# Second feed-forward: where ScalarE normalises the group three ahead

## The reference

```
x = x + 0.5 * ffn(layernorm(x))              # ffn: x @ w + bias, w = quantised kernel + a @ b
# and then, for the router of the experts, on layernorm(x):
ri = concat(xf, mean, std, min, max, l2, share of |x| < 1e-6)
h = gelu(ri @ r1_w.T + r1_b);  probs = softmax(h @ r2_w.T)
```

## Time and profile before

| | us |
|---|---|
| median of 3 runs | 1660.39 |
| lowest and highest | 1659.22, 1662.93 |
| the profiled execution | 1666.03 |
| its span, first to last instruction | 1664.2 |
| the stage of the change, in the span | about 570 to 683 |
| mean granted clock of TensorE | 0.906 |

### The profile page before, as it was taken

One profiled execution on the slowest core, in us unless ns is written; L12 is line 12 of the kernel. 1 busy time (PEld: TensorE's weight loads), 2 busy tenths in 40 slices (PEclk: granted clock), 3 DMA queues, 4 the chain that ended last, 5 costly groups with the idle time before them and its releaser, 6 DMA issues. The chain is left out here.

```text
span 1664.2 us, 26073 instructions
## 1 busy us (share of the span) xinstructions
PE 1402.3 (84%) x9264; PEld 1053.8 (63%) x9264; DVE 960.6 (58%) x2915; ACT 684.0 (41%) x1640; POOL 627.1 (38%) x573
## 2 busy tenths in 40 slices
PE   6889979999999778447999999499995459999995
PEld 5667544555554455226988899366663349888895
DVE  8987756777775488784542112266676855521120
ACT  4222147666666377434522232114333525322221
POOL 6652112221213243304435755422211232636655
PEclk9989879999999899658999999799996569999998
DMA  3034493333210023314777997611113326969985
GB/s 112 20 138 147 130 171 62 86 61 86 57 32 2 1 89 114 155 22 136 232 220 241 235 309 178 142 36 51 51 48 115 103 66 197 266 200 270 264 232 91
DMA packets 115534, 215.10 MB, mean 129 GB/s; under 512 B 20455, under 2 KB 80524, under 8 KB 106509
## 3 DMA queue, kind: packets, MB, share of 16 engines
q1 hardware_dynamic: 88526, 181.30, 34.5%
q0 software_dynamic: 26880, 32.13, 12.4%
HBM read 160.69 MB, written 52.30 MB: 128 GB/s over the span
## 5 line engine op out<-in xcount | busy, mean ns | idle before, releaser
L1072 DVE TENSOR_REDUCE attnm_top<-psum 128x1 f32<-128x63 f32 (+7 forms) x512 | 200.2, 449 | 65.4 <-PE psum L1153 62.8
L1295 ACT ACTIVATE attnm_prob<-psum 128x512 f32<-128x512 f32 (+1 forms) x384 | 189.7, 529 | 69.4 <-PE psum L1164 62.7
L2472 POOL DMA_INDIRECT out<-moe2e_y,moe_scatter_i x80 | 125.0, 1563 | 106.9 <-DMA out<-moe2e_y,moe_scatter_i 51.7
L2472 POOL DMA_INDIRECT x_sum<-moe1e_y,moe_scatter_i x80 | 125.3, 1566 | 106.0 <-DMA x_sum<-moe1e_y,moe_scatter_i 60.7
L2671 DVE SCALAR_TENSOR_TENSOR moe1e_h<-moe1e_gate,psum 128x160 f32<-128x160 f32 x160 | 50.5, 321 | 186.1 <-ACT moe1e_gate L2609 186.0
L2671 DVE SCALAR_TENSOR_TENSOR moe2e_h<-moe2e_gate,psum 128x160 f32<-128x160 f32 x160 | 50.5, 321 | 185.7 <-ACT moe2e_gate L2609 185.6
L2541 PE MATMUL psum<-moe2e_xgT,moe_w_up 128*128 128x160 f32 x1024 | 148.9, 303 | 0.8 <-ACT moe2e_xgT L2618 0.8
L2541 PE MATMUL psum<-moe1e_xgT,moe_w_up 128*128 128x160 f32 x1024 | 148.7, 302 | 0.8 <-ACT moe1e_xgT L2618 0.8
L2541 PEld LDWEIGHTS psum<-moe2e_xgT,moe_w_up 128*128 128x128 f32 x1024 | 143.9, 192 | 3.5 <-issue 2.5
L2541 PEld LDWEIGHTS psum<-moe1e_xgT,moe_w_up 128*128 128x128 f32 x1024 | 143.7, 192 | 3.5 <-issue 2.5
L1473 POOL DMA_INDIRECT moe_xg<-xn_rows,moe_gather_i x80 | 84.6, 1058 | 160.7 <-DVE moe_gather_i L1661 93.4
(11 more groups left out here) (435 smaller groups left out, 3134.7 us busy)
## 6 DMA issues: line engine op xcount, KB each, us to landing
moe_w_up<-in_expert_up SPq DMA_DIRECT2D x64, 1024.0 KB, 7.7
moe_w_down<-in_expert_down SPq DMA_DIRECT2D x64, 512.0 KB, 7.4
attnm_q_hat<-q_parts SPq DMA_DIRECT2D x72, 128.0 KB
moe_a_up<-in_adapter_up SPq DMA_DIRECT2D x32, 256.0 KB, 7.7
q_parts<-attnf_q_part SPq DMA_DIRECT2D x12, 512.0 KB, 2.8
attnm_k_hat<-k_parts SPq DMA_DIRECT2D x72, 64.0 KB
x_res<-in_x SPq DMA_DIRECT2D x8, 512.0 KB, 8.2
v_tails<-attnf_v_tail SPq DMA_DIRECT2D x8, 512.0 KB, 3.2
```

Source lines behind the costliest of these rows:

```text
L1072: ins = nc.vector.tensor_reduce(top[:, n // QUADS % 2, tile, hh:hh + 1], s.ps[:, u.bank, first:end], AX_X, ALU.max)
L1295: nc.scalar.activation(prob[:, i % NPROB, at:GROUP], s.ps[:, u.bank, at:GROUP], ACT.Exp).then_inc(taken[u.bank], 1)
L2472: nc.gpsimd.indirect_dma_start(total, bass.IndirectOffsetOnAxis(ap=scatter_i[:, at:at + 1], axis=0), y[:, q, k, :], None, bounds_check=TOK ...
```

## The change

In ScalarE's loop of `ffn_router`, `norm(i + 3)` stands directly behind `copy(i + 2)`, ahead of the router's work of the turn, instead of between `copy_x(i - 1)` and `gelu(i - 2)`. Nothing else is changed.

```diff
                 if 0 <= i + 2 < GROUPS:
                     copy(i + 2)
+                if 0 <= i + 3 < GROUPS:
+                    norm(i + 3)
                 if 0 <= i - 1 < GROUPS:
                     r.absolute(act, i - 1)
                     r.under(act, i - 1)
...
                     r.copy_s(act, i - 2)
                 if 0 <= i - 1 < GROUPS:
                     r.copy_x(act, i - 1)
-                if 0 <= i + 3 < GROUPS:
-                    norm(i + 3)
                 if 0 <= i - 2 < GROUPS:
                     r.gelu(act, i - 2)
```

## The result

| | median us | lowest, highest | runs |
|---|---|---|---|
| before | 1660.39 | 1656.73, 1662.93 | 9 |
| changed | 1665.27 | 1662.64, 1669.25 | 9 |

The ratio is 1.0041, with a 95% interval of 1.0028 to 1.0054: slower, by 4.6 to 9.0 us as the ratio has it and by 4.9 between the medians. The forecast was 1665.4. In a second job, with its own runs of the kernel before, the unedited changed kernel gave 1.0024 (1.0006 to 1.0042).

The account below looks back on a forecast made before the run. A closed ACT-PE round bounds the stage, no engine alone. C(5) at 612.0, then two turns of 12.64 + 1.54 us, put C(7) 5.0 us late: median 1660.39 becomes 1665.4, range 1660.0 to 1668.4.

Parts of the forecast that it names:

- The round: Second feed-forward with router: ACT to PE and back takes 10.57 us a turn, 12.64 with the normalisation ahead of copy_s.
- Turn 1: Group 4's normalisation fits in ACT's 3.80 us wait for DVE; C(4), its copy, comes 4.1 us earlier.
- Turn 2: Group 5's copy, C(5), at 612.0 against 613.49 before, with PE waiting 3.2 us for DVE's statistics.
- last two small operations: End of DVE's statistics of group 0: bias(5) may hold them; up to 1.2 us are covered before copy_s.
- two cases: C(5) at 610.9 with PE at full clock, or 613.1 with all behind PE's wait at half clock.
- Turns 3 and 4 and the clock: Each round lasts 12.64 us plus 1.54 for PE's fall to half clock after 2.95 us idle; C(7) 5.0 us late.
- the row with 2.94 us of waiting: PE's idle stretch before 656.86: clock fell from 2.4 to 1.2 GHz, L1938 took 3.50 us instead of 1.96.
- C: Rival: DVE paces the turns, so losing its clash with POOL gains up to 8.2 us, 1652.2; chance 0.06.
- D: Rival: the loss is taken up behind C(7), where ACT waits 2.35 us a turn; 1660.4 us, chance 0.08.
- B: Rival: PE's clock holds, C(7) is 0.8 us late, 1661.2 us, no difference that can be told; chance 0.28.

Follow-up runs that it names:

- Half the dose: The changed kernel with only tiles 0 and 1 of each group normalised ahead, 2 and 3 in the old place; turns 11.67 and 11.54 us, no ratio.
- a version with two other edits: Kernel before with groups 4, 5 normalised ahead, PE's row transposes first, POOL's powers before the bias add, router transposes repeated on PE; ratio 0.9974.

## Why the prediction was right, and where its terms were off

**The round.** Right. 0.91 + 3.89 + 0.81 + 4.96 closes without the normalisation, and with it ahead of copy_s the turn lasts 12.53 us; the sum said 12.64. Of the 0.11 us, 0.09 is that Abs starts 1.98 behind the start of L2144, not 2.07, when it need not wait (610.63 to 612.61): the term should have been the distance between the starts, not the duration. Half the dose gives half, a place behind copy_s gives nothing.

**Turn 1.** Right. C(4) is 9.64 us behind C(3) where it was 13.78, a lead of 4.1.

**Turn 2.** The total agrees, 612.0 against 609.72 + 2.50 = 612.22 on the clock of before, but in part by luck. PE's wait was put at 3.2 us and was 3.93. The "last two small operations" of the statistics were held by bias(5), L1857 taking 0.91 us, which the prediction called covered up to 1.2 us. It was covered for ACT, all but 0.38 us at copy_s, but not for PE, whose transposes wait for it: with group 4 alone ahead, without that bias add, the wait was 3.18. So the hidden layer started at 605.63 + 2.50 = 608.13, where the forecast had 606.88, or 607.5 at half clock. Against this it ran at full clock (1.98 us) behind transposes at half clock; 612.0 was the middle of two cases, and neither came. What the clock cost is an estimate, with the one turn at full clock as its measure, which comes from a version with two other edits: between 1 us (13.01 against 11.97) and 2.7 (14.65).

**Turns 3 and 4 and the clock.** This is the term that was mis-sized: +1.54 us for each was taken, by the row with 2.94 us of waiting. The fall came in turn 4 alone in both profiles of the changed kernel, and cost 1.6; behind the same 2.84 us turn 3 had none. So C(7) was 3.5 us late instead of 5.0, and the stage 3.7 us longer: the missing 1.5 is the fall of turn 3. One row of such a wait was not enough to call both.

**The time.** The medians differ by the 5 us of the forecast, while the profile's stage says 3.7, which lies below the first interval (4.6 to 9.0) and inside the second (1.0 to 7.0). How many of the turns fall in a run without a profile is not seen. A fall in turn 3 too would make C(7) 5.1 us late (an estimate, 3.5 + 1.6), and a turn 2 of 14.65 us another 1.6; against this, the stretch behind C(7) varies by up to 5 us between profiles. That falls fill the difference is argued and not shown, and that the medians meet the forecast so closely is luck, since in the profile one of its terms is missing.

**The rivals.** C failed as told: without the clash DVE only waits longer. D failed too: from C(7) to L1928 of turn 7 every profile has the same 21.5 us, early or late, and turn 5 has its 2.35 us of waiting as before (the Gelu there is 8.65 us behind C(7) in rows 4 and in both profiles of the changed kernel). B, no falls and 0.8 us, did not occur in a profile of the changed kernel. What the Trainium skill says of the shared SBUF interfaces (GPSIMD Engine Reference, Key points) agrees with the rows (L1841 3.42 us beside the bias add and 1.38 without, L1857 0.91 and 0.16). For the time it is worth nothing in turns 3 and 4, where DVE is not on the round; in turn 2, where PE waits for the statistics, it is on the path, and the 0.75 us of L1857 is PE's longer wait.

## What to carry to other kernels

In a software pipeline over several engines, add up the closed round from engine to engine and back before moving an instruction: an engine that looks 86% busy can have slack in one stretch of its turn and none in the next. An instruction in front of the one that releases the other engine costs its full time in every turn that has no wait at the new place; directly behind it, it can be free. Move ahead only the turns in which the engine waits at the new place anyway, and look at what the new waits do to TensorE's clock, which here took 1 to 2.7 us of a lead of 4.1.

## What the hardware showed

In the cases seen here, a small DVE operation that met POOL's running bias add ended 0.02 to 0.03 us behind it, however short it is otherwise (0.16 us). A copy of 128x8 (L1857) took 0.91 us in the changed kernel, where the bias add ends at 602.96 and the copy at 602.99, and 1.57 with groups 6 and 7 ahead; an operation on 128x4 with two inputs (L1829) took 2.22 with the normalisation behind copy_s. A reduction of 128x1024 beside the bias add kept its 1.21 us. Moving the bias add in time mostly chose another operation that paid; in turns 3 and 4 of the changed kernel it ran beside L2073 (1.22 us) and L94 (1.40), as long as anywhere, and nothing was slowed.

PE waits of the same 2.84 us, behind the same instructions, left the clock at 2.4 GHz in turn 3 and brought 1.2 GHz in turn 4, in two profiles out of two. What differs between the two turns is open. And the unedited end of the stage (C(7) to L2267) lasted 45.8 to 50.8 us from one execution to the next, by the clock of its last three hidden layers (1.9 to 3.8 us each), more than the whole change is worth.
